# Issuing x's transposes one stripe ahead of Q and V, and summing x in pieces, in a fused transformer layer

## What is computed

```python
q = heads(x @ Wq + bq); k = heads(x @ Wk + bk); v = heads(x @ Wv + bv)
pattern = einsum('bhid,bhjd->bhij', k, q) / 8
prob = softmax(pattern, axis=-2)
out = einsum('bhis,bhid->bhsd', prob, v)
x = layernorm(x + out @ Wo + bo)
x = layernorm(x + gelu(x @ w1 + b1) @ w2 + b2)
```

## Time and profile before

| | us |
|---|---|
| median of 2 runs | 4765.85 |
| profiled execution | 4771.16 |
| its span, slowest of 8 cores (4734.8 to 4769.6) | 4769.6 |
| PE busy | 3603.4 (76%) |
| ACT busy | 2267.7 (48%) |
| DVE busy | 1527.1 (32%) |
| mean granted clock of TensorE, cores 0 to 7 | 0.897 to 0.904 |

### The profile page before, as it was taken

One profiled execution on the slowest core, in us unless ns is written; L12 is line 12 of the kernel. 1 busy time (PEld: TensorE's weight loads), 2 busy tenths in 40 slices (PEclk: granted clock), 3 DMA queues, 4 the chain that ended last, 5 costly groups with the idle time before them and its releaser, 6 DMA issues.

```text
span 4769.6 us, 57896 instructions; the slowest of 8 cores (4734.8 to 4769.6 us)
## 1 busy us (share of the span) xinstructions
PE 3603.4 (76%) x19049; PEld 1208.0 (25%) x19264; DVE 1527.1 (32%) x1942; ACT 2267.7 (48%) x2127; POOL 302.1 (6%) x568
## 2 busy tenths in 40 slices
PE   2365569777888788878887888788878887888765
PEld 1122224122222222222222222222222222222222
DVE  1132254112424242424232423242415241524243
ACT  0000000786555655565556555655575557555600
POOL 0132220000000000000000000000000000000000
PEclk8677779999989999999999999998999999999987
DMA  8655522212332233223322332233223322332143
GB/s 165 148 142 134 130 76 75 80 54 89 87 84 82 86 89 87 80 90 89 88 80 87 91 89 80 87 90 85 80 83 93 90 80 82 92 92 77 53 93 79
DMA packets 754059, 433.81 MB, mean 91 GB/s; under 512 B 685029, under 2 KB 701541, under 8 KB 736361
## 3 DMA queue, kind: packets, MB, share of 16 engines
q1 hardware_dynamic: 708890, 237.13, 20.2%
q0 software_dynamic: 44880, 192.98, 13.4%
HBM read 377.59 MB, written 77.59 MB: 95 GB/s over the span
## 4 chain that ended last, share of the span: by engine, by line
PE 55%; ACT 13%; DVE 12%; DMA 11%; issue 6%; POOL 1%; DVEq 0%; SPq 0%; ACTq 0%; POOLq 0%
PE ps_o L781 10%; ACT es_sb L771 10%; PE ps_s L758 9%; PE ps_d L793 6%; PE ps_w L671 5%; PE ps_g L671 5%; PE ps_w L627 5%; PE ps_g L627 4%; ACT h_sb L645 2%; PE psv L333 2%; DMA wcast<-w 2%; PE psq L384 2%; DMA xt_f<-xtf_b 2%; DMA w_scr<-wcast 2%; PE psq L305 2%
## 5 line engine op out<-in xcount | busy, mean ns | idle before, releaser
L771 ACT ACTIVATE es_sb<-ps_s 128x1024 bf16<-128x1024 f32 x2048 | 2095.4, 1023 | 1325.0 <-PE ps_s L758 1169.6
L781 PE MATMUL ps_o<-es_sb,v_sb 128*64 128x512 bf16 x4096 | 860.9, 410 | 378.6 <-ACT es_sb L771 320.4
L758 PE MATMUL ps_s<-q_sb,k_sb 64*128 64x512 bf16 x4096 | 819.6, 402 | 104.1 <-DMA q_sb<-q_scr 86.3
L793 PE MATMUL ps_d<-es_sb,ones 128*64 128x512 bf16 x4096 | 839.5, 393 | 0.0
L781 PEld LDWEIGHTS ps_o<-es_sb,v_sb 128*64 128x64 bf16 x4096 | 257.7, 107 | 1032.9 <-issue 1030.0
L758 PEld LDWEIGHTS ps_s<-q_sb,k_sb 64*128 64x128 bf16 x4096 | 192.7, 93 | 972.6 <-issue 972.6
L771 ACT ACT_TABLE_LOAD x15 | 19.2, 1283 | 878.9 <-PE ps_s L758 878.4
L822 DVE COPY dD_sb<-ps_d 128x512 f32<-128x512 f32 x64 | 44.2, 691 | 855.0 <-PE ps_d L793 850.9
L671 PE MATMUL ps_w<-h_sb,w_sb 128*128 128x512 bf16 x993 | 255.7, 408 | 81.9 <-ACT h_sb L645 77.3
L627 PE MATMUL ps_w<-h1b_sb,w_sb 128*128 128x512 bf16 x986 | 256.6, 406 | 68.8 <-DVE h1b_sb L561 57.5
L305 PE MATMUL psq<-xt_bf,wq_sb 128*128 128x512 bf16 x496 | 142.3, 454 | 206.7 <-DVE q_b L313 182.4
(11 more groups left out here) (92 smaller groups left out, 2404.2 us busy)
## 6 DMA issues: line engine op xcount, KB each, us to landing
k_sb<-k_scr POOLq DMA_DIRECT2D x64, 1024.0 KB, 5.4
v_sb<-v_scr POOLq DMA_DIRECT2D x64, 1024.0 KB, 7.5
w_sb<-w_scr SPq DMA_DIRECT2D x256, 256.0 KB, 3.0
w_sb<-w_scr SPq DMA_DIRECT2D x128, 512.0 KB, 4.3
xnat<-x SPq DMA_DIRECT2D x32, 512.0 KB, 7.8
xt_f<-xtf_b SPq DMA_DIRECT2D x64, 256.0 KB, 2.2
w_scr<-wcast SPq DMA_DIRECT2D x64, 256.0 KB, 3.6
wo_sb<-wo_scr SPq DMA_DIRECT2D x64, 256.0 KB, 3.7
```

The costliest lines, as they stand in the source:

```text
L758: fn = lambda e, p=p, b=b, kc=kc, hh=hh: e.matmul(ps_s[kc % 2][:, hh * 512:(hh + 1) * 512], k_sb[b][hh * 64:(hh + 1) * 64, kc * 128:(kc + ...
L771: "act", lambda e, kc=kc, esb=esb: e.activation(es_sb[esb][:], ps_s[kc % 2][:], AF.Exp, scale=SCALE))
L781: tr.op("pe", lambda e, b=b, kc=kc, esb=esb, hh=hh: e.matmul(ps_o[hh * 64:(hh + 1) * 64, :], v_sb[b][:, kc * 128 + hh * 64: kc * 128 + (hh ...
L793: fn = lambda e, kc=kc, esb=esb, hh=hh: e.matmul(ps_d[hh * 64:(hh + 1) * 64, :], ones64[:], es_sb[esb][:, hh * 512:(hh + 1) * 512], start= ...
```

## The change

The body of the stripe loop becomes two functions. `emit_transposes(stp)` holds the x load, the transposes and their copies and stores. `emit_qv(stp)` holds Q and V. The new loop has one turn more, and in turn s issues the transposes of stripe s, up to 4 jobs, Q and V of stripe s-1, up to 3 jobs. The jobs are thus split: 4 in turn 0, 4 + 3 in turns 1 to 6, 2 in turn 7.

The sum of x is made in pieces: behind each cast DVE sums the 512 new columns into `xpart2`, and after the stripes 8 reductions of 8 elements give `xmean`. The 8 reductions of 4096 elements in the last stripe go. So does PE's wait on `pst_free_a`, whose values are 0 throughout.

```diff
-            for stp in range(nst if alvl >= 4 else 0):
+            v_xtbf_l = [0] * (NST + 1)
+
+            def emit_transposes(stp):
                 buf = stp % 2
                 tr.wait("sp", pe, stripe_pe_done[buf])
...
                     tr.wait("pe", dve, pst_free_d[tb])
-                    tr.wait("pe", act, pst_free_a[tb])
...
                         pst_free_d[tb] = vv
+                        if alvl >= 5 and sub4 >= "b":
+                            tr.op("dve", lambda e, ec=ec, stp=stp: e.reduce_sum(
+                                xpart2[:, ec * NST + stp: ec * NST + stp + 1],
+                                xt_bf[ec][:, stp * 512:(stp + 1) * 512], axis=AXX))
...
-                v_xtbf = tr.val(dve)
+                v_xtbf_l[stp] = tr.val(dve)
                 stripe_pe_done[buf] = tr.val(pe)
-                for _ in range(7):
-                    try:
-                        next(jobs_gen)
-                    except StopIteration:
-                        break
...
+            def emit_qv(stp):
...
-                    tr.wait("pe", dve, v_xtbf)
+                    tr.wait("pe", dve, v_xtbf_l[stp])
...
-                    if stp == NST - 1 and alvl >= 5 and sub4 >= "b":
-                        for ec2 in (2 * j, 2 * j + 1):
-                            tr.op("dve", lambda e, ec2=ec2: e.reduce_sum(
-                                xmean[:, ec2:ec2 + 1], xt_bf[ec2][:], axis=AXX))
...
+            nst_eff = nst if alvl >= 4 else 0
+            for stp in range(nst_eff + 1):
+                if stp < nst_eff:
+                    emit_transposes(stp)
+                    for _ in range(4):
+                        try:
+                            next(jobs_gen)
+                        except StopIteration:
+                            break
+                if stp >= 1:
+                    emit_qv(stp - 1)
+                    for _ in range(3):
+                        try:
+                            next(jobs_gen)
+                        except StopIteration:
+                            break
+
             v_xm = 0
             if alvl >= 5:
+                for ec in range(NEC):
+                    tr.op("dve", lambda e, ec=ec: e.reduce_sum(
+                        xmean[:, ec:ec + 1],
+                        xpart2[:, ec * NST:(ec + 1) * NST], axis=AXX))
```

More of the change, by code:

```diff
@@ L130, in build @@
         xmean = SB("xmean", [128, NEC], F32)
+        xpart2 = SB("xpart2", [128, NEC * NST], F32)
         xmean_b = SB("xmean_b", [128, NEC], BF16)
@@ L244, in build @@
             xtf_free = [0, 0]
-            for stp in range(nst if alvl >= 4 else 0):
+            xpart = xmean
+            v_xtbf_l = [0] * (NST + 1)
+            def emit_transposes(stp):
                 buf = stp % 2
```

## The result

The ratio of the changed kernel to the kernel before is 1.0148, 95% interval 1.013 to 1.0167: some 70 us slower. In some executions of every kernel the cores of one die run longer at a lower clock; the ratios and times in this document leave these out, and the others of the changed kernel lie at 4835.8 to 4839.7 us (before: 4757.6 to 4783.3, median 4763.0). The forecast was 4824, slower, inside 2%.

A forecast was written before the change was run, and what follows sets the result against it. Chains of waits, no full engine, bound the stripes; PE idles while SP stands at jobs. Start 181, 5 x 88.9, and the end put the K pass at 769, +58.5 us: 4824 us, range 4770 to 4880.

The forecast's parts named there:

- The stripe in full swing: Middle stripes: x load behind 3 job stores whose casts follow the V stores; 89 us a stripe instead of 74.9.
- The end: Last stripes: V(5) to V(6) 84 us, then V(6), Q(7), V(7), evacuation, tiny reductions and kap up to the K pass.
- The start: First turns, with large 1 MB jobs: V of stripe 0 starts at 181 us instead of 161.9, between 170 and 190.
- two stores at once, then one landing (5), a cast (11.3) and two more stores (2): Start: four more large jobs after the first transposes, ending at 169 us where those transposes end at 151.
- The reductions: Eight 512-element sums a stripe on DVE, 0.62 us each, 5.0 us a stripe, costed at nothing.
- Fit in that gap: Transposes: two reductions add 1.2 us to DVE's 2.3 us of work in 4.3 us, hidden while it waits for xt_f stores.
- The term for the tail: Last stripe: 8 reductions of 4.42 us, 35.4 us, leave DVE; 8 tiny ones at the end take about 2.
- The load is still covered: Rival: stripes stay at 74.9 us and only the tail's reductions are saved; -25 us, 4741 us; chance 0.07.
- The transfers collide: Rival: x load slowed beside casts and job stores, landing over 14 us; p = 95, or 98 with reductions, 4880 us; chance 0.17.
- p: Time of one stripe in full swing: forecast 89 us, ends 82 and 95; start of K pass = 236 + 6p.
- Q runs free: Rival: V(s) starts 6 us after the jobs; p = 83, +23, 4789 us; inside the forecast's own range, no separate chance.
- The signs of being wrong: x load under 25 us after V's start, K pass to end moving over 20 us, or transposes over 25 us.

The follow-up runs named there:

- e8: The changed kernel with the same three jobs taken between Q and V instead of behind V; 4702.7 to 4710.8 us, V to V 66.8.
- e4: The changed kernel with only the x load issued ahead of the three jobs behind V; ratio to the kernel before 1.0006, V to V 76.2.
- e2: The changed kernel with the old reductions of 4096 elements and without the 8 small ones, so the new order alone; ratio to the kernel before 1.0162.
- e1: The kernel before with only the sum of x made in pieces; ratio to the kernel before 0.9983.

## Why the prediction was right

**The stripe in full swing: right step by step.** From V's start, expected against the rows of the changed kernel: V stores issued 24.2 and 23.5; x load issued from 37.3 and 35.2; transposes begin 47.2 and 47.7; last xt_f store 67.1 and 66.1; q stores begin 76.9 and 76.0; next V 88.9 and 89.0. Over five stripes 89.4. e8, which only lets the three casts start ahead of the V stores, takes away 23 of the 89, and e4 shows the rest of the mechanism. That the total came out within 1 us is partly luck. The forecast had 88.9 with the reductions at nothing; without them the stripe measured 86.9 (e2), and they add 2.5. The forecast's 17.3 for the transposes came from a slow stripe of the kernel before, where e2 has 14.2; that made up for the missing cost.

**The end: nearly right.** V(5) to V(6) took 78.2, not 84 (728.4 - 650.2). I let Q begin after the last xt_f store and two jobs; it began at 711.9 behind the last transposes, 3.6 us ahead of that store, and ran 16.4 us. From V(6) to the K pass 60.5, expected 59.5.

**The start: mis-sized, and that is where the missing part lies.** I put V of stripe 0 at 181; it came at 203.0. The failed term is "two stores at once, then one landing (5), a cast (11.3) and two more stores (2)", 18 us for four large jobs. They took 35.1 (153.2 to 188.3). It let the two casts run side by side. The rows of POOL above show it: the cast at 160.4 was free 7 us after the stores began, but the next could go out only at 172.9, since the store before it, issued from 157.1 on, landed only then, beside that cast. From the third on, large jobs ran one after another, 12.4 us apart here, however early the first two casts had landed. The casts in the earlier trace rows, 12.7 us apart, already said so. The x load there was late too: issuing its four pieces took 7.4 us, not 2, and PE began at 135, not 126. The transposes won 7 of these 9 back: 18 us to the last store, not the 25 taken from stripe 1 of the kernel before. Start 22 late, five stripes 2.5 late, the end 5 early: 20 us on the K pass, which the forecast had at 769 and the trace has at 788.9. (The forecast started from core 0, whose K pass now starts at 790.8; in the mean of eight cores the start moved by 75 us, where 58.5 was forecast.)

**The reductions: cost not nothing.** "Fit in that gap" failed. I took the gap from the slowest stripe, where the stores are slow; the pace is the larger of stores and DVE work block by block. e1 and e2 measure 1 and 3 us a stripe; in the changed kernel that ate all of the tail's gain. The term for the tail, 22 us, was right. The 0.686 us of a reduction lies at the upper bound that I gave, not at the 0.62 that I took.

**The rivals.** "The load is still covered" did not occur. "The transfers collide" did so only in the first turns; in full swing p was 89, under its 95, and x landed after a median of 7.8 us in the stripe above, under its 14. (Its p with the reductions added should read 100, not 98: 94.9 + 5.) "Q runs free" occurred in part: Q's stall fell to 8 us, but the q stores, two buffers deep, still took 14.5 us behind the jobs.

**The signs of being wrong.** None came. The x load went out 35.2 us after V's start, not under 25; the transposes took 18 us, under 25; the stretch behind the K pass's start moved by 17 us on core 0, inside the 20 allowed, and by 1 us on cores 2 and 4.

## What to carry to other kernels

When an issue queue runs in written order, a prefetch is only as early as the slowest wait ahead of it, and that wait can hang on another engine's order: here SP's load waited for POOL's casts, and POOL's casts for V stores. Before work is moved for overlap, list for each queue what stands ahead of every load, and through which engine it is released; then either put the load first with all that follows it, or give the stream that waits a queue of its own (ACT: 0.9714 with no change of PE's order). Size a stall-filling edit from the stretch where the stall is smallest, not where it is largest.

## What the runs showed of the hardware

A tensor_reduce along the free dimension took 160 ns for 8 elements, 686 for 512 and 4420 for 4096: about 0.15 us and 1.04 ns an element (f32 for the 8, bf16 for the others). The Trainium skill, VectorE: DVE Perf Modes, section on the perf-mode tier table, gives it the slowest mode only. The runs agree as far as they go: the two lengths in bf16 and the one in f32 lie on one line. Cutting a sum into eight pieces costs the fixed part eight times.

SP's issue of one 512 KB load took 4.5 us at its longest in the changed kernel, beside a large cast and large stores, where the median is 0.54 us:

```profile
L256 SPq DMA_DIRECT2D xnat<-x x32: 357/538/4471, 34.4 to 688.9; - x32
```

I had treated the time of an issue as fixed.
